# Four PSUM banks of a first layer shared one to three instead of two to two, and a second layer three steps behind

## The reference, cut to what matters

```python
h1 = jnp.einsum('td,eid->tei', x2, w1)
h3 = jnp.einsum('td,eid->tei', x2, w3)
h = jax.nn.silu(h1) * h3
y = jnp.einsum('tei,edi,te->td', h, w2, cw)
z = jax.nn.silu(x2 @ sw1.T) * (x2 @ sw3.T) @ sw2.T
```

## Time and profile before

| what | value |
|---|---|
| median of three runs | 1794.09 us |
| profiled execution | 1794.41 us |
| its span | 1792.6 us |
| TensorE busy | 1509.6 us (84%) |
| VectorE busy | 1178.3 us (66%) |
| ScalarE busy | 879.1 us (49%) |
| POOL busy | 761.5 us (42%) |
| mean granted TensorE clock | 0.95 |
| DMA queue of SP, share of 16 engines | 67.6% |

### The profile page before, as it was taken

One profiled execution on the slowest core, in us unless ns is written; L12 is line 12 of the kernel. 1 busy time (PEld: TensorE's weight loads), 2 busy tenths in 40 slices (PEclk: granted clock), 3 DMA queues, 4 the chain that ended last, 5 costly groups with the idle time before them and its releaser, 6 DMA issues. The chain is left out here.

```text
span 1792.6 us, 29976 instructions
## 1 busy us (share of the span) xinstructions
PE 1509.6 (84%) x9094; PEld 1184.0 (66%) x9094; DVE 1178.3 (66%) x2060; ACT 879.1 (49%) x2809; POOL 761.5 (42%) x761
## 2 busy tenths in 40 slices
PE   1721698999899988989899988999899988999997
PEld 1201575877668765877668765777668765887686
DVE  5856686687768666667768676677768666355511
ACT  2333655556545645547535655546545644335310
POOL 4327244633373234623464243633373233733431
PEclk9955799999999989999999999999999989999998
DMA  9897777778677777777777687768777775223320
GB/s 341 358 361 276 300 276 272 276 276 291 245 280 260 281 262 268 273 275 274 256 247 297 241 292 278 276 253 299 256 263 280 268 262 158 70 64 111 96 84 24
DMA packets 127672, 440.11 MB, mean 246 GB/s; under 512 B 14221, under 2 KB 80930, under 8 KB 105998
## 3 DMA queue, kind: packets, MB, share of 16 engines
q1 hardware_dynamic: 126390, 436.79, 67.6%
q10 hardware_dynamic: 1112, 1.30, 0.3%
HBM read 413.86 MB, written 20.07 MB: 242 GB/s over the span
## 5 line engine op out<-in xcount | busy, mean ns | idle before, releaser
L752 POOL TENSOR_TENSOR ffn<-ffn 128x384 f32<-128x384 f32 (+2 forms) x448 | 510.3, 1144 | 888.7 <-ACT ffn L913 810.2
L1509 PE MATMUL bank<-W2T,ffn 128*128 128x192 f32 (+1 forms) x3600 | 705.7, 333 | 10.2 <-ACT stage L890 5.0
L1509 PEld LDWEIGHTS bank<-W2T,ffn 128*128 128x128 f32 (+1 forms) x3600 | 604.9, 191 | 79.8 <-issue 16.5
L1266 DVE TENSOR_TENSOR ffn<-bank,ffn 128x384 f32<-128x384 f32 (+2 forms) x504 | 310.4, 617 | 349.3 <-PE bank L1353 151.8
L960 DVE TENSOR_REDUCE pooled<-xt 128x3 f32<-128x768 f32 (+2 forms) x375 | 447.8, 1195 | 18.5 <-DMA xt<-in_x 17.9
L913 ACT ACTIVATE ffn<-bank 128x384 f32<-128x384 f32 (+2 forms) x504 | 272.3, 542 | 370.3 <-PE bank L1524 141.3
L801 ACT ACTIVATE xt<-xt 128x256 f32<-128x256 f32 x809 | 329.7, 414 | 83.7 <-DMA xt<-in_x 76.1
L1524 PE MATMUL bank<-X2T,Wx 126*128 126x384 bf16 (+2 forms) x720 | 202.6, 355 | 46.7 <-DVE ffn L1266 31.9
L801 ACT ACTIVATION_READ_ACCUMULATOR xt<-xt 128x1 f32 x809 | 158.6, 196 | 0.0
L1353 PE MATMUL bank<-x0h,WT0h 128*128 128x512 f32 x288 | 130.5, 453 | 6.0 <-DVE ffn L1266 6.0
L1524 PEld LDWEIGHTS bank<-X2T,Wx 126*128 126x128 bf16 x720 | 58.2, 100 | 103.7 <-DVE ffn L1266 46.1
(11 more groups left out here) (234 smaller groups left out, 1786.1 us busy)
## 6 DMA issues: line engine op xcount, KB each, us to landing
xt<-in_x SPq DMA_DIRECT2D x168, 1792.0 KB, 8.2
ffn<-cw_rows SPq DMA_DIRECT2D x192, 256.0 KB, 6.8
ffn<-cw_rows SPq DMA_DIRECT2D x192, 192.0 KB, 8.8
out<-stage SPq DMA_DIRECT2D x192, 96.0 KB
ffn<-cw_rows SPq DMA_DIRECT2D x64, 224.0 KB, 7.1
h2q<-Msb SPq DMA_DIRECT2D x64, 54.0 KB
ffn<-in_L_ffn_w SPq DMA_DIRECT2D x2, 768.0 KB
attw<-in_L_ffn_w SPq DMA_DIRECT2D x1, 512.0 KB
```

What stands on the lines that cost most here:

```text
L752: nc.gpsimd.tensor_tensor(out=cwb[slot][:, 0:n], in0=silu[(g.par + step) % 2][:, 0:n], in1=cwb[slot][:, 0:n], op=ALU.mult).then_inc(scaled, 1)
L1266: v.tensor_tensor(out=h[step % HR][:, 0:n], in0=h_ps(g, step, 1)[:, 0:n], in1=(silu[p] if e == NE else cwb[(c * NE + e) % CW_RING])[:, 0:n ...
L1509: last = mm(o, h[step % HR][:, 128 * t:128 * t + m], W2T[:, e, :], start=(e == 0 and t % 2 == 0), stop=(e == NE), skip_group_check=True)
```

## The change

The first product of every step goes to bank 0. The second product of step s goes to bank 1, 2 or 3, by s modulo 3 (`HR`). TensorE waits for silu(s), not silu(s-1), before it starts the first product of s+1. It then waits for h(s-3), issues the second layer of s-3, and after it the second product of s. Before, it waited for h(s-2), issued the second product of s and after it the second layer of s-2. Because the last second layer of a chunk comes one step later, the evacuations on ScalarE and VectorE move from the second to the third step of the next chunk. At the very end three second layers are left instead of two.

```diff
--- before.py
+++ after.py
@@ -377,7 +377,7 @@
 
         def h_ps(g, step, k):
 
-            return bank[2 * ((g.par + step) % 2) + k]
+            return bank[0] if k == 0 else bank[1 + step % HR]
 
 
 
@@ -920,7 +920,7 @@
                         silu_act(g, step + 1)
                     elif not last:
                         silu_act(g.plus(1), 0)
-                    if e == 1 and 0 < c <= QCH:
+                    if e == 2 and 0 < c <= QCH:
                         evacuate(g, c - 1)
                     step_act(g, step, left)
 
@@ -1252,9 +1252,9 @@
                 for step in range(STEPS):
                     c, e = divmod(step, EX)
                     n = CHUNKS[c][2]
-                    if e == 1 and c == QCH + 1:
+                    if e == 2 and c == QCH + 1:
                         evacuate(g, QCH)
-                    elif step == 1 and not first:
+                    elif step == 2 and not first:
                         evacuate(g.minus(1), NCH - 1)
                     p = (g.par + step) % 2
                     if e == NE:
@@ -1526,18 +1526,17 @@
 
             def ffn_pe(g, left, first=False, last=False):
                 for step in range(STEPS):
+                    wait(pe, silu_done, g.at(STEPS, step + 1))
                     if step + 1 < STEPS:
-                        wait(pe, silu_done, g.at(STEPS, step))
                         layer1(g, step + 1, 0)
                     elif not last:
-                        wait(pe, silu_done, g.at(STEPS, step))
                         layer1(g.plus(1), 0, 0)
-                    wait(pe, h_done, g.at(STEPS, step - 1))
+                    wait(pe, h_done, g.at(STEPS, step - HR + 1))
+                    if step >= HR:
+                        layer2(g, step - HR)
+                    elif not first:
+                        layer2(g.minus(1), step - HR + STEPS)
                     layer1(g, step, 1)
-                    if step >= 2:
-                        layer2(g, step - 2)
-                    elif not first:
-                        layer2(g.minus(1), step - 2 + STEPS)
                     step_pe(g, step, left)
 
             def step_pe(g, step, left):
@@ -1555,7 +1554,7 @@
             ffn_pe(G(None, 5), 2)
             ffn_pe(G(None, 6), 1)
             ffn_pe(G(None, 7), 0, last=True)
-            for step in (STEPS - 2, STEPS - 1):
+            for step in range(STEPS - HR, STEPS):
                 pe.wait_ge(h_done, G(None, 7).at(STEPS, step + 1))
                 layer2(G(None, 7), step)
```

## The result

The changed kernel takes 1880.21 us, the median of four runs (1877.12 to 1882.18). The kernel before took 1794.56 us (median of four) on the same chip. The ratio is 1.0483, with a 95% interval of 1.0436 to 1.0530: the change costs 86 us. The forecast was 1850. The profiled execution of the changed kernel took 1877.12 us, its span 1875.3. First the page: busy time of each engine, and the granted clock in 40 slices.

A forecast was written before the change was run, and what follows sets the result against it. The prediction took TensorE, busy 1509.6 of 1792.6 us, to set the pace. Terms for late silus, later second products, evacuation waits and the clock summed to +56 on 1794.4, giving 1850 us, range 1808 to 1880.

The forecast's parts named there:

- clock term: Half-speed stretches of 3.4 us after stalls at steps 6 and 7, in half of the eight groups: +7 us.
- Clock, 1875: Rival: stalls long enough to lower the clock in nearly every group, twice in some; 1875 us, chance 0.12.
- Step 7: TensorE waits for silu(7), late behind the scores' exponential and a table load, 1.99 us in seven groups: +15.1 us.
- Step 13: Silu late by 1.21 us behind the second exponential; a later transfer wait absorbs it in six groups: +2.4 us.
- Query gates: h(30) and h(31) wait for later second products, +4 us; looser h waits at steps 33 to 36 gain 0.
- Query transposes: Steps 21 and 26: normalised rows come later, queued behind h(20) and h(25): +5 us.
- Key statistics: From h(40), starting 1.5 us later, a chain without slack slips through silu(47) to step 49: +10.5 us.
- Key gates: From h(53), VectorE's queue slips, delaying U's operand, an evacuation and the last gate, 1.8 us a group: +12 us.
- Evacuation and start: Shorter waits for an evacuation at line 890, -2.0 us; first group's start behind a late silu, +1.9 us.
- only ScalarE's stalls count, 1815: Rival: late silus give 19.4 us, later second products only a few because VectorE catches up; 1815 us, chance 0.18.
- no change: Rival: silu stalls end in other waits and slips in VectorE's 193 us of waiting; about 1802 us, chance 0.08.
- faster rival: Rival: waits for h are the real bound and their 37.9 us come back; 1756 us, chance 0.04.

The follow-up runs named there:

- e5: Changed kernel with 512 unread products added in TensorE's waits (steps 7, 13, 31, the exponentials' and query gates' transposes): 1842.46 us, ratio 1.0280.
- e8: Kernel before with unread products ahead of the exponentials' transposes (8 and 4) and the query gates' (4): 1786.66 us, ratio 0.9952.
- e1: Kernel before with only the stricter wait: the first product of s+1 waits for silu(s), not silu(s-1): 1828.11 us, ratio 1.0192.
- e3: Changed kernel with two banks for each product again and the waits this needs, second layer still three behind: 1834.83 us, ratio 1.0216.
- e2: Kernel before with only the order changed: second layer of s-2 ahead of the second product of s: 1823.80 us, ratio 1.0164.
- e7: Changed kernel with VectorE's other items of a step ahead of its h, not behind it: 1826.53 us, ratio 1.0184.
- e4: Changed kernel with TensorE's transpose of the query gates at step 38 instead of 36: 1869.68 us, ratio 1.0439.
- e6: Kernel before with the transpose of the query gates at step 38 instead of 36: 1780.01 us, ratio 0.9925.
- e12: e3 with VectorE's items ahead of h and unread products ahead of the exponentials' and query gates' transposes: 1795.67 us, ratio 0.9991.

## Why the prediction was wrong in size

The sign was right, the forecast of 1850 was 30 us short, and the range ended 0.2 us below the time.

- **The clock term (7 us) failed: its size, not its mechanism.** The prediction took a single row, behind a stall of 3.4 us, and half of the groups. It counted a stretch of 3.4 us, though the row itself shows 7 us at 0.51. And its trace had the answer for shorter stalls too: behind the wait of 2.07 us of the earlier trace rows, and behind the like waits at steps 34 to 36 of six other groups, the kernel before already ran at half clock.

```profile
899.50:902.90 3.40, 2.69 (x9) 2.10 (x10) 3.19 (x11) 0.54 (x1) 0.28 (x1) 0.51 0.81 274
```

  Measured in the changed kernel: step 7 at 0.50 to 0.59 in all eight groups, and further stretches at steps 12 to 14 and 28 to 38. e5 puts it at 38 us for this kernel, 30 net of what e8 shows of the kernel before. That is above its upper end of 27, and the rival "Clock, 1875" was the nearest to what happened. The prediction had named what leads to it, a stall of 1.84 and a new one of 1.99 with one short item between, and then priced that pair as a chance of one half.
- **Step 7 (+15.1): right.** Steps 3 to 8 cost 15.9 with the clock kept up (e5), 34.0 without. The extra 18 belong to the clock.
- **Step 13 (+2.4): the mechanism is right, the agreement of the sum (-0.2) is luck.** e1 shows the mechanism by itself: 9.6 us more at step 12, that is 1.2 a group, and the transfer wait at line 1449 down from 12.0 to 0.9. In the changed kernel step 12 grew by 2.1 a group; the other 0.9 is in e3 too (7.4 in all), so it comes without the stricter wait. Read against the -9 that "no change" gives in this row, the changed kernel lost some 8 us here, and 5.4 + 2.5 of it are steps 13 and 14 at a low clock, which e5 does not have (0 at both, -8.1 in the row).
- **Query gates (+4, looser wait 0): right at full clock, 4.9.** Of the waits for h, the 31.2 us of steps 34 to 36 went as foretold, into line 1482 (23.6 more at step 36; 21.4 net of the key gates, where 25 was given as a sign) and into the silu wait ahead of step 31. The 6.0 of line 1353 stood at step 45, where silu took the place, as foretold too. What was missed is again the clock: low stretches now follow both the wait for silu at step 31 and the gate wait at step 36, in seven groups each and up to 7 us long, where the kernel before had one of 3.4 us in seven groups: 18.3 in all. The prediction also gave as a sign of error that steps 31 to 37 become shorter. They did: 926.99 to 943.61 is 16.62 against 18.05. But the 2.60 of silu wait now lies ahead of step 31; counted in, the stretch is longer, 19.22. The sign was badly cut, its mechanism holds.
- **Query transposes (+5): 6.3. Key statistics (+10.5): 9.8.** Right. h(40) starts 2.13 behind step 40's start (953.60) where it was 0.58 before, the 1.5 foretold.
- **Key gates (+12): 22.9, the forecast too small.** At step 55 the wait is 1.98, not 1.3, and the one for the evacuation grew by 1.23 (0.72 to 1.95), of which the gate wait gave back 0.4 (2.2 us in six groups) and not half: steps 53 to 59 of the group shown take 32.64 us where they took 30.07. This is 2.6 a group for the forecast 1.8. Three groups have it; three others have 4.1, with a low clock behind step 57; the last two have nothing. e2 shows it comes from the order, e7 that it comes through VectorE's queue.
- **Evacuation and start (-0.1): -8.4,** and more against the +6 of "no change" in this row. The waits for line 890 fell only from 5.0 to 4.6, not by 2. What became shorter is the wait at line 1402, 2.7 us for 10.4 before. That had no term. It goes with the order (2.5 in e2, but 9.9 in e1); why is not shown.
- **The rival that only ScalarE's stalls count, 1815,** is refuted by e2 and e7, "no change" by every run of the parts. The faster rival rested on the waits for h; they did vanish, and the waits for the gates and for silu took their place (e4). It also leaned on the page "Perfetto Trace Analysis" of the Trainium skill (Optimizing Tensor Performance, Matmuls), by which independent products rotate over banks so that reading one overlaps writing the next. e1 (one reader's wait made as strict as a single bank makes it, 35 us) and e3 (45 us less with two and two) agree with that for the first products; no run shows a gain from three banks for the second ones.

The decomposition adds up: 7.3 us of the table's sum of 82.7 is the later start of step 0 of the first group (the wait for its first silu, which stood ahead of step 1 before), the other 75.4 the steps, and the medians differ by 86 because the profiled execution of the changed kernel was its fastest.

**Left open.** Why line 1402 waits less. Why the transfer at line 1449 is awaited for 8 to 18 us in runs whose edits do not touch it (12.0 before, 8.4 in e6, 10.8 in e8, 18.3 in e12). And how the clock's 30 us divide over the two parts of the change, since no run filled e1 or e2.

## What to carry to other kernels

When a change adds a stall to TensorE, look for the other stalls within a few microseconds of it and for what stalls of that length do to the clock elsewhere in the same trace: price the work behind them at half clock in every repetition where the trace does so, and check with products that nobody reads. A buffer given from one product to another moves a wait, it does not remove it: ask which engine is next in line for the buffer left single. Then ask what that engine itself waits for: here silu(37) waited for VectorE. And an operation issued later on TensorE delays everything queued behind its reader, so follow that reader's queue and not only its next result; before more buffers are tried, see whether the last wait of the stretch can be asked for later, which was the one cheap gain here.

## What was not expected of the hardware

- Around two stalls of 1.84 and 1.73 us with 0.8 us of work between them the granted clock of TensorE was 0.51 for 7 us (852.20 to 859.20), and step 7 was slow in every group. With the first stall alone it was 1.00 there in all groups of the kernel before, but not in all of e2, which has the same stall of 1.84 and another order of products: in two of its eight groups the clock fell less than 2 us behind it. So a single stall of this length can do it, and what else decides is not shown.

```profile
627.20:630.40 3.20, 3.20 (x17) 2.47 (x15) 1.61 (x3) 3.19 (x11) 0.99 (x1) 0.50 0.17 57
```

- 512 additional matmuls made the changed kernel 38 us faster, and 128 made the kernel before 8 to 9 us faster. In e6 they did not help: 1785.4 with, 1780.0 without.
- A product (1 - mean clock) x span gives a quick bound of the loss to the clock: 133 us in the changed kernel, 90 before, 72 in e5. The difference of 61 between the changed kernel and e5 is above the 38 us gained, since part of the slow time was waiting.
- The table load ahead of silu(7) takes 1.28 us, and the activation starts 1.30 behind its start here too.
